# A transformer tower on one core: order of the router's preparation on TensorE and VectorE between fusion and the first expert

## The chip, the cores and the metric

One core of a Trainium2 chip runs the whole program. The time is device microseconds of that core for one launch, input in device memory to output in device memory; the median of several runs counts.

## The reference

A small vision tower in float32 over 16 images, 36 tokens each (T = 576 tokens of width 256), in five steps: patch embedding; a bidirectional minGRU stack of four layers, fused to width 256; a mixture of eight experts of which each token uses two; causal attention of 8 heads; a ternary MLP. The change lies between the fusion and the experts, where this is computed:

```python
h = h + L0_attn(layernorm(h))            # ends with: einsum(h_comb, fusion_W) + fusion_b
x = layernorm(h).reshape(T, 256)
probs = softmax(x @ gate_w.T)            # 8 experts
w, idx = top_k(probs, 2)
w = w / sum(w)
combine = zeros((T, 8)).at[rows, idx].add(w)
for each expert: acc += combine[:, e] * (silu(g) * u @ down.T)   # g, u = split(x @ up.T)
h = h + acc
```

## The kernel before, in words

Activations lie transposed: 128 partitions hold features, two blocks `k` for 256, and the free axis holds tokens. Tokens are worked in two halves of NT = 288, and where tokens must be on partitions in six tiles `j` of 96, three for each half. Every engine has an order written out by hand, and semaphores tie them together; `wait_ge(s, n)` stops the engine's queue until s has reached n. Nothing is scheduled by a tool.

A layer norm number i is a chain over four engines. `ln_mean(i)` on TensorE multiplies a half by a matrix of 1/256, so that every partition has the mean; VectorE's `ln_center(i)` (L1248) subtracts it; ScalarE's `squares(i)` (L1021) squares; `ln_square(i)` (L513) sums squares into three columns of 96 tokens; VectorE's `ln_eps(i)` (L1257) adds epsilon; GpSimd's `power(i)` (L410) raises to -0.5. For the two halves before the experts, i = LN_MOE and LN_MOE + 1, the result `rmoe` isn't multiplied into the activations: tokens are centred only, and the scale of each token is applied to its logits (`prs`) and, by ScalarE (L1080), to its row. `ln_square(i)` also waits until `s_ve` has reached i, that is until `ln_eps(i - 1)` is done; `ln_eps(i)` waits for its sums and for `power(i - 2)`.

The stretch of the change, in the order in which the engines run it:

- TensorE: `fuse(n, k)` (L598), the fusion product of half n with its k-th block of features, 4 passes for each k. The mean products of both halves (L499), `logits(0)` (L680), squares of half 0, `logits(1)`, squares of half 1, twelve transposes that put the centred tokens on partitions (L694), six products of zeros (`stay_warm`, L494), then the products of the ranks (L702 to L704), nine more products of zeros, and `gather_first` (L713).
- VectorE: `add_fused(n)` (L1358) adds the fusion into `h`; centering; the selection of two experts for each token (L1379 to L1396); the combine weights (L1401 to L1404, semaphore `s_comb`); from the ranks the seats (L1408), the row numbers `place` (L1412), and six masks `first` (L1417), with which `gather_first` picks the tokens of expert 0 by a product, without memory in between.
- ScalarE: the exponentials of the scaled logits (L1074), and six copies of the scaled token rows into `xtok` (L1080), for which `gather_first` waits.
- GpSimd: twelve indirect DMAs (L446) scatter the rows, with their combine weights behind them, to device memory; it waits for `s_place`, `s_comb` and the copies. Only behind all twelve (`s_move`) does SyncE load the rows of experts 1, 0 and 2 (L333), and behind these the up weights of expert 2 (L321).

The experts follow: `up` (L747), `down` (L764), and `turn_up(x)` (L723), which transposes the loaded rows of expert x. That of expert 1 stands in the middle of `down(0)`:

```python
for m in range(KH):
    for k in range(KI):
        last = pe.matmul(bank[:, 7, m * C:(m + 1) * C], wdn[i][:, k, m * P:(m + 1) * P], ...)
    if m == 0 and x == 0:
        turn_up(c, 1)
```

For x from 3 on, SyncE loads expert x's rows behind its down weights, which wait for the end of `down(x - 2)`.

Of the kernel before, what the change touches and what calls it, by code (L numbers as in the profile page):

```python
# [9 lines left out]
ALU = mybir.AluOpType  # L10
ACT = mybir.ActivationFunctionType
AX_X = mybir.AxisListType.X

P = 128
B, S = 16, 36
T = B * S
H = 256
# [41 lines left out]
def tower(nc, patches, w_tok, w_gru, w_fus, vecs, w_gate, w_up, w_down, w_qkv, w_gates, w_o, w_1, w_2, slots, mixed, out):  # L59
    with ExitStack() as ctx:  # L60
# [135 lines left out]
        def half(n):  # L196
            return slice(n * NT, (n + 1) * NT)
# [291 lines left out]
        def _(pe):  # L489
# [6 lines left out]
            def ln_mean(i, src):  # L496

                for k in range(KH):
                    last = pe.matmul(bank[:, mean_bank(i), 0:NT], avg[:], src[:, k, :], start=(k == 0), stop=(k == KH - 1))  # L499
                last.then_inc(s_mean, 1)  # L500
# [172 lines left out]
            fuse(1, 2)  # L673
            fuse(1, 3)
# [8 lines left out]

            pe.wait_ge(s_load["wr"], 16)
            for n in range(2):
                pe.wait_ge(s_hf, n + 1)
                ln_mean(LN_MOE + n, h[:, :, half(n)])
            logits(0)
            ln_square(LN_MOE)
            logits(1)  # L690
            ln_square(LN_MOE + 1)
            for j in range(6):
                for m in range(KH):
                    last = pe.transpose(bank[0:TT, j // 2, j % 2 * H + m * P:j % 2 * H + (m + 1) * P],  # L694
                                        xn[:, m, j * TT:(j + 1) * TT], ident[:])
                if j % 2 == 1:
                    last.then_inc(s_xtp, 1)

            stay_warm(6, 3)
# [521 lines left out]
        def _(dve):  # L1221
# [144 lines left out]
            for n in range(2):  # L1366
                ln_center(LN_MOE + n)
            ln_eps(LN_MOE)
# [4 lines left out]
            def by_tile(x):  # L1373
# [11 lines left out]
            ln_eps(LN_MOE + 1)  # L1385
# [5 lines left out]
            dve.wait_ge(s_pow, LN_MOE + 2)  # L1391
            dve.tensor_tensor(prs[:], pr[:], over(rmoe), ALU.mult).then_inc(s_max, 1)
# [7 lines left out]
            dve.wait_ge(s_exp, 1)  # L1400
            link(dve, dve.tensor_tensor(ex[:], ex[:], msk[:], ALU.mult))  # L1401
            link(dve, dve.tensor_reduce(den[:], by_tile(ex[:]), AX_X, ALU.add))
            link(dve, dve.reciprocal(den[:], den[:]))
            dve.tensor_tensor(xtok[:, :, H + 1:ROW], by_tile(ex[:]),  # L1404
                              den[:].rearrange("p (j o) -> p j o", o=1).broadcast_to([TT, 6, E]), ALU.mult).then_inc(s_comb, 1)
# [12 lines left out]

            link(dve, dve.tensor_reduce(rone[:], bank[0:1, 7, 6 * E:7 * E], AX_X, ALU.max))
# [215 lines left out]
```

## Time and profile before

| | |
|---|---|
| median of 3 runs | 430.42 us (429.53 to 431.42) |
| profiled execution, its own time | 425.62 us |
| its span, first to last instruction | 423.8 us |
| mean granted clock of TensorE | 0.974 |
| TensorE products busy | 397.4 us (94%) |
| TensorE weight loads busy | 334.1 us (79%) |
| VectorE / ScalarE / GpSimd busy | 206.1 / 147.7 / 104.1 us |

The span is that of one execution under the profiler, and the time beside it is that execution's. Busy TensorE time counts pipelined products from their start to a modelled end, so it says little on how fast it works; the clock and the chain of waits say more. The stretch of the change takes some 20 us from 120 on.

### The profile page before, as it was taken

What the parts mean: (1) busy time and instruction counts of PE and PEld (TensorE: products, weight loads), DVE (VectorE), ACT (ScalarE), POOL (GpSimd) and SP (SyncE); (2) the same over time, 40 slices, a digit from 0 to 9 for tenths busy, and PEclk for the clock granted to TensorE, in tenths of its full rate; (3) what the DMA queues carried; (4) which work ended last, traced back from release to release, by engine and by line L of the source; (5) the groups of instructions that cost most, each with busy time, mean ns of one, the idle gap of its engine ahead of it and who ended that gap; (6) DMA issues with size and microseconds to landing.
All of it is one profiled execution on the core that took longest, in us unless ns stands there. A gap on an engine that the chain in (4) does not pass through costs nothing.

```text
span 423.8 us, 6446 instructions
## 1 busy us (share of the span) xinstructions
PE 397.4 (94%) x2482; PEld 334.1 (79%) x2482; DVE 206.1 (49%) x438; ACT 147.7 (35%) x314; POOL 104.1 (25%) x126
## 2 busy tenths in 40 slices
PE   8999999999999989999899998986999888999895
PEld 5787887888778889989799898984867555679783
DVE  0347688888945334253333424320213997435452
ACT  1045666666315212121111212110164444346542
POOL 2014544454311731120202202022010040003440
PEclk9999999999996999999899999996999999999989
DMA  7999992000000247768376574013600000000001
GB/s 236 354 318 283 354 394 84 1 2 0 2 0 2 67 115 290 227 141 300 49 291 184 164 236 107 2 19 58 223 0 2 0 2 2 2 0 2 0 2 56
DMA packets 31348, 48.43 MB, mean 114 GB/s; under 512 B 2128, under 2 KB 28368, under 8 KB 29264
## 3 DMA queue, kind: packets, MB, share of 16 engines
q1 hardware_dynamic: 28944, 45.17, 32.7%
q0 software_dynamic: 2368, 2.80, 4.4%
q8 instruction: 21, 0.34, 0.3%
q14 instruction: 15, 0.12, 0.1%
HBM read 38.90 MB, written 9.05 MB: 113 GB/s over the span
## 4 chain that ended last, share of the span: by engine, by line
PE 74%; DMA 8%; DVE 7%; issue 4%; ACT 4%; SPq 2%; POOL 1%; POOLq 0%
PE bank L747 14%; PE bank L617 14%; PE bank L764 10%; DMA wg<-slots 7%; PE bank L499 6%; PE bank L494 4%; PE bank L513 4%; PE bank L973 3%; PE bank L565 2%; PE bank L832 2%; PE bank L894 2%; PE bank L598 2%; PE bank L535 2%; PE bank L959 1%; PE bank L882 1%
## 5 line engine op out<-in xcount | busy, mean ns | idle before, releaser
L747 PE MATMUL bank<-tt,wup 128*128 128x192 f32 x512 | 88.6, 331 | 0.7 <-ACT tt L1090 0.7
L747 PEld LDWEIGHTS bank<-tt,wup 128*128 128x128 f32 x512 | 84.7, 193 | 0.9 <-issue 0.9
L1428 DVE TENSOR_TENSOR scratch<-bank,scratch 128x192 f32<-128x192 f32 x64 | 22.8, 356 | 88.0 <-ACT scratch L1105 88.0
L457 POOL DMA_INDIRECT mixed<-wg,token x16 | 22.6, 1412 | 116.3 <-DVE wg L1442 113.9
L617 PE MATMUL bank<-gru_x,wg 128*128 128x288 f32 x192 | 50.8, 408 | 0.0
L1105 ACT ACTIVATE scratch<-bank 128x192 f32<-128x192 f32 x64 | 21.2, 331 | 73.0 <-PE bank L747 73.0
L410 POOL TENSOR_TENSOR rm<-ve,half_neg 96x3 f32<-96x3 f32 x24 | 21.0, 874 | 96.5 <-DVE ve L1257 89.7
L617 PEld LDWEIGHTS bank<-gru_x,wg 128*128 128x128 f32 x192 | 35.5, 190 | 8.8
L429 POOL TENSOR_TENSOR sq<-sq 128x288 f32<-128x288 f32 x14 | 26.0, 1855 | 23.9 <-ACT sq L1021 23.9
L494 PE MATMUL bank<-zero 128*128 128x288 bf16 x155 | 26.5, 323 | 4.7 <-issue 3.5
L494 PEld LDWEIGHTS bank<-zero 128*128 128x128 bf16 x155 | 16.7, 111 | 11.1 <-issue 3.7
L513 PEld LDWEIGHTS bank<-mean_h,sq 128*96 128x96 f32 x204 | 21.5, 171 | 3.0 <-DVE fbias L1337 0.5
L764 PE MATMUL bank<-gru_x,wdn 128*128 128x192 f32 x128 | 21.9, 329 | 1.3 <-DVE gru_x L1430 1.3
L764 PE MATMUL bank<-gru_y,wdn 128*128 128x192 f32 x128 | 21.8, 328 | 1.3 <-issue 1.3
L764 PEld LDWEIGHTS bank<-gru_x,wdn 128*128 128x128 f32 x128 | 20.7, 190 | 2.2 <-issue 2.2
L764 PEld LDWEIGHTS bank<-gru_y,wdn 128*128 128x128 f32 x128 | 20.7, 190 | 2.2 <-issue 2.2
L513 PE MATMUL bank<-mean_h,sq 128*96 128x1 f32 x204 | 20.5, 222 | 0.0
L1021 ACT ACTIVATE sq<-xn 128x576 f32<-128x576 f32 x8 | 5.5, 682 | 42.7 <-DVE xn L1248 42.7
L1048 ACT ACTIVATE aa<-bank,nbz 128x288 f32<-128x288 f32 x32 | 14.3, 497 | 16.6 <-PE bank L617 16.6
L1248 DVE TENSOR_TENSOR gru_y<-gru_y,bank 128x576 f32<-128x576 f32 x16 | 12.1, 753 | 15.6 <-PE bank L499 15.6
L499 PE MATMUL bank<-gru_y,avg 128*128 128x288 f32 x64 | 19.5, 427 | 0.1
L821 PE MATMUL bank<-xn,xp 128*128 128x288 f32 x64 | 16.9, 413 | 2.0 <-ACT gru_y L1141 1.2
(217 smaller groups left out, 644.0 us busy)
## 6 DMA issues: line engine op xcount, KB each, us to landing
wup<-w_up SPq DMA_DIRECT2D x8, 2048.0 KB, 8.9
wdn<-w_down SPq DMA_DIRECT2D x8, 1024.0 KB, 6.7
slots<-empty SPq DMA_DIRECT2D x2, 2385.0 KB, 20.2
wg<-w_gru SPq DMA_DIRECT2D x4, 1024.0 KB, 10.8
wup<-w SPq DMA_DIRECT2D x2, 1024.0 KB, 9.3
wg<-slots SPq DMA_DIRECT2D x16, 99.4 KB, 5.3
xp<-w_qkv SPq DMA_DIRECT2D x1, 1536.0 KB, 16.8
xp<-patches SPq DMA_DIRECT2D x2, 432.0 KB, 6.1
```

The source lines that it names most:

```text
L410: pool.tensor_tensor(root, ve[i % 2][:], half_neg[0:TT, :], ALU.pow).then_inc(s_pow, 1)
L429: pool.tensor_tensor(sq[i % 2][:, 0, :], sq[i % 2][:, 0, :], sq[i % 2][:, 1, :], ALU.add).then_inc(s_pre, 1)
L457: pool.indirect_dma_start(out=mixed, out_offset=bass.IndirectOffsetOnAxis(ap=token[i][:, u:u + 1], axis=0), in_=yw[i][:, u, :], in_offset= ...
L494: pe.matmul(bank[0:rows, b, 0:NT], zero16[:, 0:rows], zero16[:], start=True, stop=True)
L499: last = pe.matmul(bank[:, mean_bank(i), 0:NT], avg[:], src[:, k, :], start=(k == 0), stop=(k == KH - 1))
L513: last = pe.matmul(bank[0:TT, stat_bank(i), j:j + 1], sq[i % 2][:, k, j * TT:(j + 1) * TT], mean_h[:], start=(k == 0), stop=(added or k == ...
L617: last = pe.matmul(bank[:, 2 * g + m, 0:NT], wg[:, l, d, g, k, m * P:(m + 1) * P], src, start=(k == 0), stop=(k == KH - 1))
L747: last = pe.matmul(bank[:, 2 + m % 4, g * 256:g * 256 + C], wup[i][:, k, g * I + m * P:g * I + (m + 1) * P], xg[i][:, k, :], start=(k == 0 ...
L764: last = pe.matmul(bank[:, 7, m * C:(m + 1) * C], wdn[i][:, k, m * P:(m + 1) * P], act[i][:, k, :], start=(k == 0), stop=(k == KI - 1))
L821: last = pe.matmul(bank[:, head_bank(q), 0:NT], wqkv[:, k, c * 512 + m * P:c * 512 + (m + 1) * P], xn[:, k, half(n)], start=(k == 0), stop ...
L1105: sc_.activation(sg[m % 2], bank[:, 2 + m % 4, 0:C], ACT.Sigmoid).then_inc(ps[c]["sig"], 1)
L1428: dve.tensor_tensor(gt[m % 2], bank[:, 2 + m % 4, 0:C], sg[m % 2], ALU.mult).then_inc(s_vact[c], 1)
```

## The change

Three things are moved; no operation is added or removed but two of the products of zeros.

- TensorE: the mean product of half 0 goes between the last two fusion products of half 1, behind a wait for `add_fused(0)`. `logits(0)` comes ahead of the mean product of half 1; then the transposes of half 0, `logits(1)`, both squares, and the transposes of half 1. Four products of zeros follow instead of six.
- VectorE: `add_fused` and `ln_center` alternate by half. `ln_eps` of each half moves back: that of half 0 from ahead of the logits to behind the first choice, that of half 1 to behind the second mask.
- VectorE: `prs`, the scaled logits, goes behind the selection, and the four operations of the combine weights go behind the six masks.

```diff
--- before.py
+++ after.py
@@ -671,6 +671,8 @@
             fuse(1, 1)
             pe.wait_ge(s_norm, LN_MOE)
             fuse(1, 2)
+            pe.wait_ge(s_hf, 1)
+            ln_mean(LN_MOE, h[:, :, half(0)])
             fuse(1, 3)
 
             def logits(n):
@@ -681,22 +683,25 @@
                                          start=(k == 0), stop=(k == KH - 1))
                 last.then_inc(s_logit, 1)
 
+            def rows(n):
+                for j in range(n * JT, (n + 1) * JT):
+                    for m in range(KH):
+                        last = pe.transpose(bank[0:TT, j // 2, j % 2 * H + m * P:j % 2 * H + (m + 1) * P],
+                                            xn[:, m, j * TT:(j + 1) * TT], ident[:])
+                    if j % 2 == 1:
+                        last.then_inc(s_xtp, 1)
+
             pe.wait_ge(s_load["wr"], 16)
-            for n in range(2):
-                pe.wait_ge(s_hf, n + 1)
-                ln_mean(LN_MOE + n, h[:, :, half(n)])
             logits(0)
+            pe.wait_ge(s_hf, 2)
+            ln_mean(LN_MOE + 1, h[:, :, half(1)])
+            rows(0)
+            logits(1)
             ln_square(LN_MOE)
-            logits(1)
             ln_square(LN_MOE + 1)
-            for j in range(6):
-                for m in range(KH):
-                    last = pe.transpose(bank[0:TT, j // 2, j % 2 * H + m * P:j % 2 * H + (m + 1) * P],
-                                        xn[:, m, j * TT:(j + 1) * TT], ident[:])
-                if j % 2 == 1:
-                    last.then_inc(s_xtp, 1)
-
-            stay_warm(6, 3)
+            rows(1)
+
+            stay_warm(4, 3)
             pe.wait_ge(s_msk, 1)
             flat = lambda x: x[:].rearrange("p e j -> p (e j)")
             pe.matmul(bank[0:TT, 7, 0:6 * E], not_before[:], flat(msk), start=True, stop=False)
@@ -1363,9 +1368,7 @@
             dve.wait_ge(s_fb, 1)
             for n in range(2):
                 add_fused(n)
-            for n in range(2):
                 ln_center(LN_MOE + n)
-            ln_eps(LN_MOE)
 
             def over(x):
                 return x[:].rearrange("p (o j) -> p o j", o=1).broadcast_to([TT, E, 6])
@@ -1382,14 +1385,13 @@
                                                op0=ALU.is_equal, op1=ALU.mult))
             link(dve, dve.tensor_reduce(mx1[:], by_tile(keys[:]), AX_X, ALU.max))
             link(dve, dve.tensor_tensor(sel[:, 0], keys[:], over(mx1), ALU.is_equal))
-            ln_eps(LN_MOE + 1)
+            ln_eps(LN_MOE)
             link(dve, dve.scalar_tensor_tensor(out=dest[:, 0], in0=sel[:, 0], scalar=MASKED, in1=pr[:],
                                                op0=ALU.mult, op1=ALU.add))
             link(dve, dve.tensor_reduce(mx1[:], by_tile(dest[:, 0]), AX_X, ALU.max))
             link(dve, dve.tensor_tensor(keys[:], dest[:, 0], over(mx1), ALU.is_equal))
             link(dve, dve.tensor_tensor(keys[:], keys[:], ranks[:], ALU.mult))
-            dve.wait_ge(s_pow, LN_MOE + 2)
-            dve.tensor_tensor(prs[:], pr[:], over(rmoe), ALU.mult).then_inc(s_max, 1)
+            ln_eps(LN_MOE + 1)
             link(dve, dve.tensor_reduce(mx1[:], by_tile(keys[:]), AX_X, ALU.max))
             link(dve, dve.tensor_tensor(sel[:, 1], keys[:], over(mx1), ALU.is_equal))
             link(dve, dve.tensor_tensor(msk[:], sel[:, 0], sel[:, 1], ALU.add))
@@ -1397,12 +1399,8 @@
                                    msk[:].rearrange("p e j -> p (e j)"), 0.0, ALU.mult, ALU.add).then_inc(s_msk, 1)
 
 
-            dve.wait_ge(s_exp, 1)
-            link(dve, dve.tensor_tensor(ex[:], ex[:], msk[:], ALU.mult))
-            link(dve, dve.tensor_reduce(den[:], by_tile(ex[:]), AX_X, ALU.add))
-            link(dve, dve.reciprocal(den[:], den[:]))
-            dve.tensor_tensor(xtok[:, :, H + 1:ROW], by_tile(ex[:]),
-                              den[:].rearrange("p (j o) -> p j o", o=1).broadcast_to([TT, 6, E]), ALU.mult).then_inc(s_comb, 1)
+            dve.wait_ge(s_pow, LN_MOE + 2)
+            dve.tensor_tensor(prs[:], pr[:], over(rmoe), ALU.mult).then_inc(s_max, 1)
             dve.wait_ge(s_rank, 1)
             seats = bank[0:TT, 7, 0:6 * E].rearrange("p (e j) -> p e j", j=6)
             link(dve, dve.tensor_tensor(keys[:], seats, first_slot[:], ALU.add))
@@ -1416,6 +1414,12 @@
             for j in range(6):
                 dve.tensor_scalar(first[:, j, :], seat_row, seat0[:, j:j + 1], None, ALU.is_equal).then_inc(s_first, 1)
 
+            dve.wait_ge(s_exp, 1)
+            link(dve, dve.tensor_tensor(ex[:], ex[:], msk[:], ALU.mult))
+            link(dve, dve.tensor_reduce(den[:], by_tile(ex[:]), AX_X, ALU.add))
+            link(dve, dve.reciprocal(den[:], den[:]))
+            dve.tensor_tensor(xtok[:, :, H + 1:ROW], by_tile(ex[:]),
+                              den[:].rearrange("p (j o) -> p j o", o=1).broadcast_to([TT, 6, E]), ALU.mult).then_inc(s_comb, 1)
             link(dve, dve.tensor_reduce(rone[:], bank[0:1, 7, 6 * E:7 * E], AX_X, ALU.max))
             dve.tensor_scalar(flag[:], rone[:], float(C) + 0.5, None, ALU.is_gt).then_inc(s_flag, 1)
```

## Rows read from the trace of the kernel before

**Rows 1.** Chain of waits, 120 to 142 us: start us, length us, what it was.
```profile
120.35 4.41 PE bank L598 x18
...
124.78 0.95 DVE h L1358 x2
...
125.78 1.24 PE bank L499 x4
127.02 0.94 PE bank L680 x12
127.96 1.01 PE bank L513 x12
128.97 1.92 PE bank L680 x12
...
132.81 2.64 PE bank L694 x12
135.44 0.92 PE bank L494 x6
...
137.92 4.15 PE bank L713 x24
```

**Rows 2.** Chain of waits, 179 to 211 us, same columns.
```profile
179.41 5.27 DMA wg<-slots
...
185.28 5.23 PE bank L747 x32
...
203.94 6.91 PE bank L747 x32
```

**Rows 3.** Windows, TensorE: length, busy (count), granted clock, DMA share, GB/s.
```profile
127.00:128.80 1.80, 1.80 (x25) 1.00 0.00 0
128.90:135.60 6.70, 6.70 (x39) 0.50 0.01 2
```

**Rows 4.** Timeline of VectorE, 127 to 139 us: start, length, instruction, idle before it.
```profile
127.05 0.75 DVE L1248 TENSOR_TENSOR xn<-h,bank 128x576 f32<-128x576 f32 x1 [0.55 <-PE bank L499]
...
131.00 0.20 DVE L1379 TENSOR_REDUCE mx<-bank 96x6 f32<-96x48 f32 x1 [1.83 <-PE bank L680]
...
132.90 0.16 DVE L1257 TENSOR_SCALAR ve<-bank 96x3 f32<-96x3 f32 x1 [0.71 <-PE bank L513]
...
133.48 0.20 DVE L1389 TENSOR_TENSOR keys<-dest,mx 96x48 f32<-96x48 f32 x1
...
134.09 0.20 DVE L1392 TENSOR_TENSOR prs<-pr,rmoe 96x48 f32<-96x48 f32 x1 [0.17 <-POOL rmoe L410]
...
135.13 0.18 DVE L1401 TENSOR_TENSOR ex<-ex,msk 96x48 f32<-96x48 f32 x1
...
136.50 0.20 DVE L1408 TENSOR_TENSOR keys<-bank,first_slot 96x48 f32<-96x48 f32 x1 [0.43 <-PE bank L704]
...
137.02 0.32 DVE L1412 TENSOR_REDUCE place<-dest 96x12 int32<-96x96 f32 x1
...
137.45 1.46 DVE L1417 TENSOR_SCALAR wg<-wg,seat 96x192 f32<-96x192 f32 x6
```

**Rows 5.** Timeline of ScalarE, the six copies of the token rows.
```profile
134.48 2.26 ACT L1080 ACTIVATE wg<-bank,rmoe 96x256 f32<-96x256 f32 x6
```

**Rows 6.** Timeline of GpSimd, both powers and the first two scatters.
```profile
129.25 0.85 POOL L410 TENSOR_TENSOR rmoe<-ve,half_neg 96x3 f32<-96x3 f32 x1 [9.41 <-DVE ve L1257]
133.14 0.85 POOL L410 TENSOR_TENSOR rmoe<-ve,half_neg 96x3 f32<-96x3 f32 x1 [3.04 <-DVE ve L1257]
...
138.27 1.24 POOL L446 DMA_INDIRECT slots<-wg,place  x1 [3.88 <-DVE place L1412]
139.81 0.95 POOL L446 DMA_INDIRECT slots<-wg,place  x1 [0.30 <-issue]
```

**Rows 7.** SyncE's second load of expert rows: length ns, start; time to landing.
```profile
L333 SPq DMA_DIRECT2D wg<-slots x1: 427/427/427, 155.1 to 155.1; - x1
...
DMA to landing us min/median/max: 2.1/2.1/2.1
```

**Rows 8.** Timeline of TensorE's weight loads at `turn_up(1)`.
```profile
157.27 0.38 PEld L723 LDWEIGHTS bank<-ident,wg 96*128 96x128 f32 x4
```


## The prediction

> **What bounds the kernel now.** I read the chain of waits first, from the fusion products to the experts [rows 1]: TensorE works without a pause except for one handover at 124.76, then waits for VectorE before the first gather at 137.92. The chain then stays on TensorE until 179.41, where it runs through a load of expert rows [rows 2]. So the change sits on the path. The windows show the clock [rows 3]: full speed (2.4 GHz) until 128.8, granted 0.50 (1.2 GHz) from 128.9 to 135.6, after TensorE had run fusion and mean products and then the narrow products of router and squares. At half speed twelve pairs of the router take 1.92 us, at full speed 0.94 [rows 1].
>
> Beside this chain there is a second path. GpSimd's twelve scatters start at 138.27 [rows 6]. SyncE loads the rows of expert 1 behind the last of them: its second load is issued at 155.1 and lands 2.1 us later, about 157.23 [rows 7]. TensorE takes those rows at 157.27 [rows 8], without having stood still. The two paths meet with 0.04 us of slack. What the gather gains alone is therefore lost at `turn_up(1)`, in the middle of `down(0)`; what the scatters lose is paid in full, because the later row loads follow the end of `down` [rows 2].
>
> **The change, first at full clock.** The fusion's last 18 passes take 4.41, so four take 0.98 [rows 1]. The mean product of half 0, put before `fuse(1, 3)`, moves the fusion's end from 124.76 to 125.74. `add_fused(1)` takes 0.95 and the mean of half 1 1.24 [rows 1]: 128.0. Centering takes 0.75 [rows 4]: 128.8. The first six transposes lie under it: twelve took 2.64 at half clock, so six take 0.66 at full. `logits(0)` lies under the addition. `logits(1)` follows: 0.94 and some 0.2 to fill an idle engine, 129.95, and VectorE starts its maximum at 130.05 instead of 131.00 [rows 4]. That is 0.95 gained, partly because the clock had fallen before.
>
> From there VectorE runs as before: five operations from 131.00 to 132.19 (132.90 less the 0.71 idle) take 1.19 [rows 4]. Now `ln_eps(LN_MOE)` stands behind them, and `ln_square(LN_MOE + 1)` waits for it, since a square of i waits until `s_ve` is i. This is a wait that the change adds. The first squares end at 129.95 + 1.01 = 130.96 [rows 1], the epsilon at 131.40, so the second squares run from 131.45 to 132.46, and behind them wait `rows(1)`, the warm products and the ranks. VectorE's next four take 1.02 (132.90 to 134.09 less 0.17), until 132.26; `ln_eps(LN_MOE + 1)` then waits for the second squares until 132.55. The selection up to the scan takes 134.09 to 135.20, of which 0.13 was `prs`, now moved behind: 0.98 and 0.08 for the epsilon, so the scan ends at 133.61, 1.6 sooner. On TensorE six transposes end at 133.1 and four warm products near 133.7 (six took 0.92 [rows 1]; two fewer are hidden, since the scan is as late). The ranks cost between 0.14 (end of the warm products to VectorE's 136.50) and 0.45 more; I take 0.45, as nothing is queued ahead. VectorE forms the seats at 134.1, against 136.50: 2.4 sooner.
>
> Now the moved combine weights. Before, their four operations ran from 135.13 to 136.07, in the wait for the ranks, and cost nothing [rows 4]; the idle after them was 0.43. Now they follow the six masks. From seats to places is 0.84, to the first mask 0.95, the masks 1.46, the weights 0.93: 137.4. GpSimd waits for both places and weights. Before, places were last (137.34) and the first scatter began 0.93 later. Now weights are last, 2.4 to 2.5 behind places: 137.4 + 0.93 = 138.35, against 138.27. The 2.4 us won are all spent.
>
> The gather does gain: the second power is ready at 132.55 + 0.16 + 0.90 = 133.6 [rows 6], `prs` starts near 133.65; from `prs` at 134.09 to the end of the six row copies were 134.48 + 2.26 - 134.09 = 2.65 [rows 4, 5], so 136.3, and the gather starts at 136.5, 1.4 sooner. TensorE would want the rows of expert 1 at 155.85; they come at 157.3. Net at full clock against the profiled execution: +0.04, nothing.
>
> **At half clock**, if it falls near 128.9 as it did [rows 3]: `logits(1)` ends at 128.85 + 0.2 + 1.92 = 130.97, VectorE's five at 132.24. The first squares (1.9) end at 132.9, the epsilon at 133.16, the second squares at 135.1 (before: 132.81), the scan at 136.26. Six transposes at 0.22 end at 136.4, four warm products by 137.1, seats come at 137.4 (+0.9), weights at 140.75, the first scatter at 141.65: +3.4. The gather loses 1.1. Net +3.4.
>
> **Equal clocks at full speed.** The profiled execution of before is not its best. With the clock up: `logits(1)` 128.97 to 129.9, second squares 130.9, scan near 133.4, weights 134.35, twelve transposes and six warm products 133.0, seats 134.35, first scatter 134.35 + 0.84 + 0.93 = 136.1. Against 138.35 that is +2.2. So the cost is 2.2 to 3.4 wherever both kernels have the same clock, and 0 where only the changed one keeps it.
>
> **A rule against the row.** The two powers on GpSimd took 0.85 each, the first with VectorE idle, the second (133.14 to 133.99) beside VectorE's two-input operations, of which one at 133.48 took its usual 0.20 [rows 4, 6]. By this both powers may lie beside VectorE's selection for nothing, and the sum stays. The Trainium skill, "SBUF — State Buffer", section "SBUF: two separate sides", has VectorE's operations with two SBUF inputs and a GpSimd operation that reads SBUF lock one pair of ports against each other, the later one blocked. By that rule each power would hold VectorE up by at most 0.85, and the sum would be up to 1.7 more. This trace does not agree with it for these sizes.
>
> **Other unknowns.** The first scatter took 1.24, the later ones 0.95 [rows 6]; it ran beside the masks, which it no longer does: -0.3 to 0, I take 0. That TensorE stops 1.4 at `turn_up(1)` may move where the clock falls later: one stretch of 32 up products took 6.91 where the same work took 5.23 [rows 2], so -1.7 to +1.7; I take 0.
>
> **The rivals.** A, the forecast: the clock is alike in both kernels, and the weights behind the masks put the scatters later: +2.2 to +3.4. I take +2.5, nearer the full-clock sum, since that is the state of most of the span. Chance 0.50.
> B, not slower: the wide products now put among the narrow ones keep the clock up past the second squares where before it fell at 128.9: 0 to +1. For it: a mean product and six transposes now stand between the two router products. Against: the squares and `logits(1)` are still narrow and adjacent, some 3 us with the added wait. It decides from the point where seats come 2.4 us sooner. Chance 0.30.
> C, faster: B's clock, the scatter 0.3 shorter, and a later fall of the clock gone, 1.7: -2.0 or a little more. Chance 0.11.
> D, much slower: the clock falls late and comes back only inside the gather, whose 4.15 at full clock [rows 1] then cost up to 1.7 more, on top of +3.4: +5.1. Fewer warm products (four for six) speak for it; that the scatters bind and not the gather hides most of it. Chance 0.06. The port rule of above would give 2.5 + 1.7 = +4.2, chance 0.03.
>
> **The numbers.** The profiled execution took 425.62 us for a span of 423.8, 4.8 below the median of the runs, 430.42. The sum is a difference and is put on the median: 430.42 + 2.5 = 432.9 (the profiled one would be 428.1). 0.5% is 2.15 us, about what a measurement can tell from no change. Range: from B's 0 with 1.1 for the spread of the runs shown (429.3) to A's upper end, +3.4, with 1.0 (434.8); it leaves out most of C and of D. A's own range is 432.4 to 434.0. Slower by over 0.5%: A, less a little at its lower edge, and D with the port rule: 0.52. Faster: part of C, with noise: 0.09. Within: B, the rest of C and A's edge: 0.39.
>
> **What would show it.** Seats near 134.1 at full clock or 137.4 at half; the weights' four operations right behind the masks; the first scatter 0.9 behind the weights, not the places; a gap before the squares of LN_MOE + 1; TensorE idle 1 to 2 us before `turn_up(1)`, on expert rows. I am wrong if TensorE does not wait there, or if the first scatter starts before 137.

## The result, and the profile after

The changed kernel's median is 432.05 us (428.75 to 436.77, 20 runs) against 429.43 us (424.66 to 436.59, 20 runs) of the kernel before, timed side by side: a ratio of 1.0065, with a 95% interval of 1.0036 to 1.0094. That is 2.6 us slower; the forecast was 432.9 us, +2.5. Medians here take all executions; ratios and their intervals leave out those that ran some per cent longer at a lower granted clock. The profiled execution took 428.75 us for a span of 427.0. All later times are those of that execution unless a label stands beside them; lines of kernel.py have moved by up to five (the router's products L682, epsilon L1262, seats L1406, places L1410, masks L1415, ranks L707 to L709, gather L718, `turn_up` L728, `up` L752, `down` L769).

The chain of waits of the changed kernel, 123 to 166 us (start, length, what), answers to [rows 1]:

```profile
123.95 0.97 PE bank L499 x4
124.92 0.97 PE bank L598 x4
...
129.01 1.20 PE bank L682 x12
...
131.82 1.92 PE bank L513 x12
...
138.41 4.17 PE bank L718 x24
...
150.61 6.31 another core or an unknown queue
...
160.30 4.82 PE bank L769 x14
```

The handover that stood at 124.76 is filled, and `logits(1)` starts at 129.01 and ends at 130.21. In spite of that the gather starts 0.5 us later than before (138.41 against 137.92), and a piece of 6.31 us that belongs to no engine's work stands in the middle of `up(0)`; before had none. TensorE's timeline shows the added wait, and its windows (length, busy time of TensorE, weight loads, VectorE, ScalarE and GpSimd, granted clock, DMA share, GB/s) the clock, as in [rows 3]:

```profile
130.06 1.16 PE L513 MATMUL bank<-mean_h,sq 128*96 128x1 f32 x12
131.82 1.92 PE L513 MATMUL bank<-mean_h,sq 128*96 128x1 f32 x12 [0.61 <-DVE ve L1262]
```

```profile
127.00:131.90 4.90, 4.10 (x36) 3.52 (x36) 2.14 (x9) 1.97 (x2) 0.14 (x1) 1.00 0.00 0
132.00:138.70 6.70, 6.70 (x36) 5.57 (x36) 3.96 (x20) 3.49 (x8) 1.86 (x4) 0.50 0.01 2
```

The second squares waited 0.61 us for `ln_eps(LN_MOE)`, and the clock went from 2.4 to 1.2 GHz right at their start, 3.1 us later than before, for about as long as before (6.7 us). VectorE and GpSimd, against [rows 4] and [rows 6]:

```profile
130.31 0.20 DVE L1382 TENSOR_REDUCE mx<-bank 96x6 f32<-96x48 f32 x1 [1.35 <-PE bank L682]
...
131.52 0.16 DVE L1262 TENSOR_SCALAR ve<-bank 96x3 f32<-96x3 f32 x1
...
133.84 0.16 DVE L1262 TENSOR_SCALAR ve<-bank 96x3 f32<-96x3 f32 x1 [1.30 <-PE bank L513]
...
136.27 0.20 DVE L1406 TENSOR_TENSOR keys<-bank,first_slot 96x48 f32<-96x48 f32 x1 [1.10 <-PE bank L709]
...
136.79 0.32 DVE L1410 TENSOR_REDUCE place<-dest 96x12 int32<-96x96 f32 x1
...
137.22 1.46 DVE L1415 TENSOR_SCALAR wg<-wg,seat 96x192 f32<-96x192 f32 x6
138.60 0.20 DVE L1418 TENSOR_TENSOR ex<-ex,msk 96x48 f32<-96x48 f32 x1
...
139.32 0.24 DVE L1421 TENSOR_TENSOR wg<-ex,den 96x48 f32<-96x48 f32 x1
```

```profile
131.76 0.85 POOL L410 TENSOR_TENSOR rmoe<-ve,half_neg 96x3 f32<-96x3 f32 x1 [11.74 <-DVE ve L1262]
134.08 0.85 POOL L410 TENSOR_TENSOR rmoe<-ve,half_neg 96x3 f32<-96x3 f32 x1 [1.47 <-DVE ve L1262]
...
140.54 1.18 POOL L446 DMA_INDIRECT slots<-wg,place  x1 [5.21 <-DVE wg L1421]
142.02 0.96 POOL L446 DMA_INDIRECT slots<-wg,place  x1 [0.30 <-issue]
```

Seats are 0.23 sooner than before (136.27 against 136.50), the first scatter is 2.27 later (140.54 against 138.27). It now begins 4.27 us behind the seats instead of 1.77, and its releaser is the last of the moved weights' operations, no longer the places. GpSimd stood idle 5.21 us before it instead of 3.88; what the moved weights add is the 2.5 us by which the distance from the seats grew.

The wait forecast at `turn_up(1)` does not show: its products run at 165.76, right behind the first half of `down(0)`. `down(0)` was late itself, and its first half was slow:

```profile
160.30 5.46 PE L769 MATMUL bank<-gru_x,wdn 128*128 128x192 f32 x16 [6.43 <-DVE gru_x L1434]
```

```profile
160.30:165.70 5.40, 5.40 (x17) 5.31 (x18) 0.00 (x0) 0.00 (x0) 0.00 (x0) 0.50 0.97 343
```

Before, the same sixteen products took 2.84 us. Here TensorE had stood idle for 6.43 us, and the granted clock in them was 0.50. ScalarE's sigmoids in `up(0)` say why `down(0)` came late:

```profile
146.11 0.33 ACT L1110 ACTIVATE scratch<-bank 128x192 f32<-128x192 f32 x1 [0.97 <-issue]
147.70 0.33 ACT L1110 ACTIVATE scratch<-bank 128x192 f32<-128x192 f32 x1 [1.26 <-PE bank L752]
150.59 0.33 ACT L1110 ACTIVATE scratch<-bank 128x192 f32<-128x192 f32 x1 [2.56 <-PE bank L752]
156.94 0.33 ACT L1110 ACTIVATE scratch<-bank 128x192 f32<-128x192 f32 x1 [6.03 <-remote]
157.73 0.75 ACT L1110 ACTIVATE scratch<-bank 128x192 f32<-128x192 f32 x2 [0.45 <-remote]
```

They should follow each other every 1.3 us, as they did before. Instead ScalarE stands for 6.03 us although TensorE had finished all of `up(0)` at 153.87, and `down(0)` begins at 160.30. The last scatter was issued at 154.44. I had not foreseen this, so the experiments had two questions: what part of the change holds the scatters, and by which way a late scatter costs time.

### The profile page after: what moved, and what is told of

The parts are those of the page before. It is cut to its first block, busy times and chain, and to the rows that moved or that the text cites. A ratio compares the mean times of both kernels' runs of the same rounds, so it can differ in the third digit from the quotient of the medians.

```text
span 427.0 us, 6441 instructions
## 1 busy us (share of the span) xinstructions
PE 394.0 (92%) x2480; PEld 332.2 (78%) x2480; DVE 206.0 (48%) x438; ACT 147.6 (35%) x314; POOL 104.3 (24%) x126
## 4 chain that ended last, share of the span: by engine, by line
PE 72%; DMA 8%; DVE 7%; issue 4%; ACT 4%; SPq 2%; another core or an unknown queue 2%; POOL 1%; POOLq 0%; DVEq 0%
PE bank L617 14%; PE bank L752 13%; PE bank L769 11%; DMA wg<-slots 6%; PE bank L499 6%; PE bank L494 4%; PE bank L513 4%; PE bank L565 2%; PE bank L978 2%; PE bank L837 2%; PE bank L899 2%; PE bank L598 2%; PE bank L535 1%; PE bank L887 1%
## 5 line engine op out<-in xcount | busy, mean ns | idle before, releaser
L752 PE MATMUL bank<-tt,wup 128*128 128x192 f32 x512 | 86.9, 327 | 0.7 <-ACT tt L1095 0.7
L752 PEld LDWEIGHTS bank<-tt,wup 128*128 128x128 f32 x512 | 83.1, 190 | 0.9 <-issue 0.9
L457 POOL DMA_INDIRECT mixed<-wg,token x16 | 22.6, 1413 | 120.9 <-DVE wg L1446 118.5
L769 PE MATMUL bank<-gru_x,wdn 128*128 128x192 f32 x128 | 24.6, 354 | 6.4 <-DVE gru_x L1434 6.4
L494 PE MATMUL bank<-zero 128*128 128x288 bf16 x153 | 25.0, 312 | 4.9 <-issue 3.6
L769 PEld LDWEIGHTS bank<-gru_x,wdn 128*128 128x128 f32 x128 | 23.1, 208 | 7.3 <-issue 7.3
L494 PEld LDWEIGHTS bank<-zero 128*128 128x128 bf16 x153 | 15.8, 107 | 10.2 <-issue 3.9
L769 PE MATMUL bank<-gru_y,wdn 128*128 128x192 f32 x128 | 21.8, 328 | 1.3 <-issue 1.3
L769 PEld LDWEIGHTS bank<-gru_y,wdn 128*128 128x128 f32 x128 | 20.7, 190 | 2.2 <-issue 2.2
```

The lines of the kernel that those rows point to most:

```text
L457: pool.indirect_dma_start(out=mixed, out_offset=bass.IndirectOffsetOnAxis(ap=token[i][:, u:u + 1], axis=0), in_=yw[i][:, u, :], in_offset= ...
L494: pe.matmul(bank[0:rows, b, 0:NT], zero16[:, 0:rows], zero16[:], start=True, stop=True)
L752: last = pe.matmul(bank[:, 2 + m % 4, g * 256:g * 256 + C], wup[i][:, k, g * I + m * P:g * I + (m + 1) * P], xg[i][:, k, :], start=(k == 0 ...
```

## The experiments

Each group ran on a chip of its own, interleaved with the kernel before. Before's medians were 429.29 us (35 runs) beside the first group, 422.75 us (29) beside the second and 430.1 us (29) beside the third. All kernels compute the whole reference.

### First group: which part costs

`r_after` is the changed kernel again.

> The changed kernel once more, for a second profile. In its first profile ScalarE stood still for 6.0 us in the middle of up(0) (150.9 to 156.9), with its inputs ready. If that stall belongs to the change, it is there again at the same sigmoid. If it is an accident of one execution, ScalarE runs every 1.3 us there, and TensorE waits instead at turn_up(1) for the rows of expert 1, 1 to 2 us. The first scatter starts 3.1 to 3.3 us behind VectorE's seats minus places, that is 4.2 us behind the seats (before: 1.8). Time against before: +0.3 to +1.0%.

Measured: 430.48 us, ratio 1.0047 (1.0009 to 1.0085). Here the clock stayed up through the second squares, so this is the forecast's full-clock walk as a measurement:

```profile
130.34 0.20 DVE L1382 TENSOR_REDUCE mx<-bank 96x6 f32<-96x48 f32 x1 [1.35 <-PE bank L682]
...
133.93 0.26 DVE L1398 TENSOR_TENSOR_SCAN incl<-tile_reset,msk 96x48 bf16<-96x48 bf16 x1
...
134.68 0.20 DVE L1406 TENSOR_TENSOR keys<-bank,first_slot 96x48 f32<-96x48 f32 x1 [0.25 <-PE bank L709]
...
137.74 0.23 DVE L1421 TENSOR_TENSOR wg<-ex,den 96x48 f32<-96x48 f32 x1
```

The first scatter starts at 138.95: 4.27 behind the seats again. The gather starts at 136.93 but takes 6.15 us instead of 4.15: the window from 137 to 142.5 has a mean granted clock of 0.64. The stall was there again: ScalarE stood 5.27 us, until its sigmoid at 155.89, and `down(0)` began at 160.36.

`e_comb_early` is the changed kernel with the weights back ahead of the ranks.

```diff
             dve.tensor_tensor(prs[:], pr[:], over(rmoe), ALU.mult).then_inc(s_max, 1)
+            dve.wait_ge(s_exp, 1)
+            link(dve, dve.tensor_tensor(ex[:], ex[:], msk[:], ALU.mult))
...
             dve.wait_ge(s_rank, 1)
```

> The changed kernel with one thing undone: the four operations of the combine weights stand ahead of the wait for the ranks again, behind prs. Theory (the weights behind the masks put the scatters later): the first scatter starts 1.8 us behind the seats instead of 4.2, so 2.4 us sooner than in the changed kernel at the same clock; the time falls to before or below it, -0.5 to 0%, 2 us less than the changed kernel. Rival (TensorE's order costs, by the wait for ln_eps or by the clock): the time stays where the changed kernel's is, +0.3 to +0.9%.

Measured: 431.72 us, ratio 1.0017 (0.9965 to 1.0068). Seats 135.27, first scatter 137.03, so 1.76 behind the seats: the 2.5 us of distance belong to the weights' place and to nothing else. They are not all won back, though. The weights now stand ahead of the seats and hold them up: from VectorE's maximum to the seats are 5.28 us (4.34 in `r_after`), and from the maximum to the first scatter 7.04 (8.61 in `r_after`). So putting the weights back is worth 1.6 us at this clock, not the 2.4 expected. The median does not come down, the ratio does; this group alone does not settle the time. The stall is here too, but TensorE has work in it, and the first half of `down(0)` keeps its speed:

```profile
158.13 2.84 PE L769 MATMUL bank<-gru_x,wdn 128*128 128x192 f32 x16 [1.29 <-DVE gru_x L1434]
```

`e_comb_late` is the kernel before with only that one move.

```diff
-            dve.wait_ge(s_exp, 1)
-            link(dve, dve.tensor_tensor(ex[:], ex[:], msk[:], ALU.mult))
...
             for j in range(6):
                 dve.tensor_scalar(first[:, j, :], seat_row, seat0[:, j:j + 1], None, ALU.is_equal).then_inc(s_first, 1)
+            dve.wait_ge(s_exp, 1)
+            link(dve, dve.tensor_tensor(ex[:], ex[:], msk[:], ALU.mult))
...
```

> The kernel before with one thing done: the four operations of the combine weights stand behind the six masks. Theory: the first scatter starts 4.2 us behind the seats instead of 1.8, but the seats can come up to 0.9 us sooner where the ranks are ready before the weights end; +1.5 to +2.4 us, +0.35 to +0.55%. Rival (TensorE's order costs): 0 within 0.2%.

Measured: 429.94 us, ratio 1.0047 (1.0005 to 1.0088). Up to the scan its timeline of VectorE is also the kernel before's at a full clock:

```profile
130.14 0.20 DVE L1379 TENSOR_REDUCE mx<-bank 96x6 f32<-96x48 f32 x1 [0.94 <-PE bank L680]
...
132.54 0.20 DVE L1392 TENSOR_TENSOR prs<-pr,rmoe 96x48 f32<-96x48 f32 x1 [0.17 <-POOL rmoe L410]
...
134.16 0.20 DVE L1402 TENSOR_TENSOR keys<-bank,first_slot 96x48 f32<-96x48 f32 x1 [0.50 <-PE bank L704]
...
134.68 0.32 DVE L1406 TENSOR_REDUCE place<-dest 96x12 int32<-96x96 f32 x1
```

With the clock up VectorE's maximum is at 130.14 in the old order and 130.34 in the new. The "0.95 gained" of the forecast was all clock. What the kernel before does at this clock can be worked out from it. The scan starts at 133.41, and the ranks are ready at 134.16. With the weights in their old place the seats stand 1.03 behind the scan where nothing waits (133.24 and 134.27 in `e_ranks_first`). That gives seats at 134.44 and the first scatter 1.77 later, at 136.2; here it starts at 138.42. Against `r_after`'s 138.95 the whole change costs the scatters 2.7 us where both clocks are up until the squares are through, 2.2 of them for the weights' place and 0.5 for the new orders of the rest. These sums rest on one profile of each kernel.

The same profile answers for the gather. `prs` is at 132.54 here and at 134.23 in `r_after`, since the change puts it behind the selection, and ScalarE's six copies of the rows wait for it. They end at 135.19 here and at 136.88 in `r_after`, and the gather follows at 136.02 and 136.93. At equal clocks the changed kernel's gather is thus not sooner but some 0.9 us later.

`e_te_only` has TensorE's new order and VectorE's old one.

```diff
             fuse(1, 2)
+            pe.wait_ge(s_hf, 1)
+            ln_mean(LN_MOE, h[:, :, half(0)])
             fuse(1, 3)
...
             logits(0)
-            ln_square(LN_MOE)
+            pe.wait_ge(s_hf, 2)
+            ln_mean(LN_MOE + 1, h[:, :, half(1)])
+            rows(0)
             logits(1)
+            ln_square(LN_MOE)
             ln_square(LN_MOE + 1)
```

> TensorE's order of the changed kernel with VectorE's order of before, so that ln_eps of half 0 stands ahead of the logits and no wait is added for the second squares. Theory: the weights are ready in the wait for the ranks, the first scatter starts 1.8 us behind the seats; -2 to 0 us, -0.45 to 0%. Rival (TensorE's order costs): +0.3 to +0.9%.

Measured: 431.34 us, ratio 1.0061 (1.0021 to 1.0102). The expectation missed how the two orders mesh. TensorE waits 1.79 us for the centering before `logits(0)` (127.69, since both additions now come first), and VectorE's maximum waits behind `ln_eps(LN_MOE)`, whose squares now stand behind `logits(1)`: 133.08 instead of 130.34. Seats come at 137.64, the first scatter 1.77 behind them at 139.41. The expectation of -0.45 to 0% was missed. The two orders are worth something only together; as a split of the cost this run says nothing.

### Second group: how a late scatter costs

`r_before` is the kernel before under a second name, to see how far apart two timings of one kernel lie.

> The kernel before once more, for a second profile. Five of six profiles so far (all but the one of before) show ScalarE standing still for 4 to 6 us inside up(0) while the scatters run, and going on as they end. Theory 1: the stall belongs to the stretch and comes in before's executions too; down(0) then starts about 20 us behind the first scatter, near 156 to 158, not at 154.7. Theory 2: the stall belongs to the change (or to what it shares with its parts); then it is absent here again and ScalarE runs every 1.3 us. If the clock holds through the second squares, the first scatter starts near 136.0 (138.3 at half clock). Time: 0 within 0.4%.

Measured: 421.92 us, ratio 0.9955 (0.9915 to 0.9996). The interval leaves out 1 for the same kernel. Ratios here are thus good to about 0.5%, not to the 0.4% that their intervals show, and I rest no verdict on a single one below that. First scatter 137.89, gather 137.72, sigmoids every 1.3 us, `down(0)` at 154.28, `turn_up(1)` at 157.12 without a wait.

`x_scatter_late` is the kernel before with the scatters held until all sigmoids of expert 0 are done.

```diff
             pool.wait_ge(s_id, 2)
+            pool.wait_ge(ps[0]["sig"], KI)
             for j in range(6):
```

> The kernel before, with GpSimd's scatters held until ScalarE has done its eight sigmoids of up(0). If the scatters in flight are what holds ScalarE up, its sigmoids run every 1.3 us here without a stall, and the stall may show up later, beside the scatters. If not, the stall of 4 to 6 us stands in up(0) as before. The time is some 12 to 17 us longer, as the rows of expert 1 come that much later.

Measured: 443.35 us, one run. Its chain of waits:

```profile
168.52 2.42 DMA slots<-wg,place
170.95 0.34 SPq L333
...
171.34 2.10 DMA wg<-slots
...
173.48 0.90 PE bank L724 x4
174.39 4.08 PE bank L765 x16
```

Scatters, landing, row load and `turn_up(1)` follow each other without a gap. First scatter 16.8 us later, `turn_up(1)` 16.4 us later, the whole some 20 us slower (12 to 17 were expected): the second path of the forecast, at its full price once its slack is gone. Some 2 us of the rest lie right there: the granted clock was 0.50 from 165 to 173.4, while TensorE stood idle, and `turn_up(1)` and the sixteen products behind it took 0.90 and 4.08 us instead of 0.35 and 2.63. ScalarE did not stall, but no kernel of this group did, so this run doesn't say whether the scatters cause the stall.

`e_turn_late` is the changed kernel with `turn_up(1)` behind `down(0)` instead of in its middle.

```diff
-                    if m == 0 and x == 0:
-                        turn_up(c, 1)
                 last.then_inc(ps[c]["dmm"], 1)
+                if x == 0:
+                    turn_up(c, 1)
```

> The changed kernel with turn_up(1) behind down(0) instead of in its middle. That gives the scatters 2.6 us more and costs about 1 us at the start of up(1), where TensorE waits for ScalarE's copy. If TensorE waits at turn_up(1) for the rows, this takes 1 to 1.5 us off the changed kernel. If ScalarE's stall sets the start of down(0) and the rows are there by then, it adds 1 us: +0.2 to +0.3% on the changed kernel.

Measured: 424.51 us, ratio 1.005 (1.0016 to 1.0084). Without a stall its timeline of TensorE reads:

```profile
153.59 5.44 PE L769 MATMUL bank<-gru_x,wdn 128*128 128x192 f32 x32 [1.30 <-DVE gru_x L1434]
158.87 0.50 PE L728 MATMUL bank<-ident,wg 96*128 96x96 f32 x4
159.99 2.84 PE L752 MATMUL bank<-tt,wup 128*128 128x192 f32 x16 [0.62 <-issue]
...
177.95 1.46 PE L752 MATMUL bank<-tt,wup 128*128 128x192 f32 x8
```

The gather began 1.0 us sooner than in `r_before` (136.72 against 137.72) and `down(0)` 0.7 sooner, and after two experts TensorE is 0.13 us behind it (the last row is at 177.82 there). That lead is one of clocks: in `r_before` the clock had fallen at 130.2, here at 133.5, and at equal clocks there is none (`e_comb_late`). It is lost here all the same, though not by the forecast's wait: the first scatter is at 138.78, so by [rows 6, 7] the rows are there at about 157.7, before `turn_up(1)` at 158.87. In its place TensorE stands 0.62 us between the turned rows and their first product. In the unmoved order TensorE would have wanted them at 153.59 + 2.84 = 156.4 and stood 1.3 us; that is worked out, and no profile shows it.

The unmoved changed kernel did not run on this chip, so the ratio says what this kernel costs and not what the move of `turn_up(1)` is worth.

`e_no_eps_wait` is `e_comb_early` without the added wait of the second squares.

```diff
                     pe.wait_ge(s_sq, i + 1)
-                if i >= 1:
+                if i >= 1 and i != LN_MOE + 1:
                     pe.wait_ge(s_ve, i)
```

> The changed kernel with the combine weights back ahead of the ranks, and without the wait of the second squares for ln_eps of the first half (they write another bank than the first). Theory: the 0.6 us of TensorE idle before the second squares is gone, the selection ends 0.5 us sooner, and the first scatter starts 0.4 to 0.6 us sooner than in the kernel with the weights alone put back (137.0 at full clock): 136.5. Still 0.5 behind before at the same clock (136.0). Time: -0.4 to +0.2% against before.

Measured: 421.41 us, ratio 0.9981 (0.9948 to 1.0015). Both squares are now one stretch of 24 products and VectorE doesn't idle at the second epsilon:

```profile
130.18 2.18 PE L513 MATMUL bank<-mean_h,sq 128*96 128x1 f32 x24
```

```profile
133.51 0.25 DVE L1398 TENSOR_TENSOR_SCAN incl<-tile_reset,msk 96x48 bf16<-96x48 bf16 x1
...
135.21 0.19 DVE L1412 TENSOR_TENSOR keys<-bank,first_slot 96x48 f32<-96x48 f32 x1
```

The scan is 0.4 us sooner than in `r_after` (133.51 against 133.93), so the added wait was worth that much. The seats are not sooner, since the weights, now ahead of them, wait for the exponential behind `prs`. First scatter 136.97, where 136.5 was expected.

### Third group: the same again on a third chip, and a version of my own

`r_after2`, `e_comb_early2` and `e_comb_late2` are `r_after`, `e_comb_early` and `e_comb_late` unchanged.

> The changed kernel a third time. On the chip of the second group no kernel showed ScalarE's stall, on that of the first group all did. Without the stall: TensorE waits at turn_up(1) for rows, 1.3 to 2 us; first scatter 4.2 us behind the seats (138.9 at full clock through the squares, up to 141 with the clock down); +0.4 to +0.8% against before. With the stall: down(0) starts near 160 again.

> The weights back ahead of the ranks, again, beside the changed kernel on one chip. Theory (the weights' place is the main cost): 1.9 us before the changed kernel at the same clock, scatter 1.8 behind the seats; -0.1 to +0.3% against before, and below the changed kernel by 0.3 to 0.5%. Rival (TensorE's order is the main cost): within 0.1% of the changed kernel.

> The kernel before with the weights alone moved behind the masks, again. Theory: its first scatter stands 4.2 us behind the seats; the wait at turn_up(1) is there with TensorE's old order too, 2 us at full clock; +0.4 to +0.5%. Rival: 0 within 0.2%.

Measured: `r_after2` 431.54 us, 1.0024 (0.9989 to 1.006); `e_comb_early2` 431.48 us, 0.9968 (0.9925 to 1.001); `e_comb_late2` 432.74 us, 1.0019 (0.9975 to 1.0062). The profiled execution of `e_comb_early2` took 437.46 us at a granted clock of 0.959, so only distances inside it are read. In `r_after2` the clock was down from the second squares on, as in the changed kernel's first profile. The whole stretch lies 1.6 us later than in `r_after`, since fourteen fusion products ahead of it took 4.51 us instead of 3.42 (maximum at 131.96 against 130.34), so it is read from the maximum on:

```profile
133.48 2.05 PE L513 MATMUL bank<-mean_h,sq 128*96 128x1 f32 x12 [0.61 <-DVE ve L1262]
```

```profile
138.05 0.20 DVE L1406 TENSOR_TENSOR keys<-bank,first_slot 96x48 f32<-96x48 f32 x1 [1.10 <-PE bank L709]
```

```profile
142.33 1.18 POOL L446 DMA_INDIRECT slots<-wg,place  x1 [5.21 <-DVE wg L1421]
...
156.19 0.94 POOL L446 DMA_INDIRECT slots<-wg,place  x1 [0.30 <-issue]
```

`e_ranks_first` is the kernel before with the rank products put ahead of the last four transposes, and without the six warm products.

```diff
-            stay_warm(6, 3)
+            rows(range(4))
             pe.wait_ge(s_msk, 1)
...
             pe.matmul(bank[0:TT, 7, 6 * E:7 * E], ones16[:], incl[:, :, 5], start=True, stop=True).then_inc(s_rank, 1)
+            rows(range(4, 6))
```

> The kernel before, with the products of the ranks ahead of the last four transposes and without the six products of zeros. In both profiles of before VectorE stood 0.4 and 1.0 us before the seats, since TensorE was still at transposes and zeros. Theory (the scatters set the pace): the seats come right behind the weights, the first scatter 0.4 to 1.0 us sooner, and the gather, which then waits for the later row copies, no later than before; -0.25 to -0.1%. If the missing zeros let the clock stay down in the gather, up to +0.5%.

Measured: 426.17 us in six runs, ratio 0.99 (0.9844 to 0.9956), four times the most that was expected and the only one below before by more than two timings of one kernel differ. The ranks are out of the queue's way:

```profile
130.74 1.89 PE L695 MATMUL bank<-ident,xn 128*96 128x128 f32 x8
133.55 0.27 PE L703 MATMUL bank<-msk,not_before 96*96 96x48 bf16 x1 [0.92 <-DVE incl L1398]
```

```profile
133.41 0.18 DVE L1403 TENSOR_TENSOR ex<-ex,msk 96x48 f32<-96x48 f32 x1
...
134.12 0.23 DVE L1406 TENSOR_TENSOR wg<-ex,den 96x48 f32<-96x48 f32 x1
134.27 0.19 DVE L1410 TENSOR_TENSOR keys<-bank,first_slot 96x48 f32<-96x48 f32 x1
```

TensorE now waits 0.92 us for the scan, where the old order made VectorE wait for TensorE. The weights fill the ranks' time, the seats follow them at once, and the first scatter starts at 136.03. That is 6.06 us behind the maximum, against 7.27 and 7.66 in the two profiles of before, and 6.1 worked out above for before at a full clock: what the new place of the ranks saves is the wait for TensorE at the low clock. The run changes two things, the place of the ranks and the six products of zeros, and does not tell them apart; nor do the 1.2 to 1.6 us explain all of the 1%.

### What the runs say together

| | maximum | clock falls at | seats | first scatter | behind seats |
|---|---|---|---|---|---|
| before | 131.00 | 128.9 | 136.50 | 138.27 | 1.77 |
| `r_before` | 130.23 | 130.2 | 136.12 | 137.89 | 1.77 |
| `e_comb_early` | 129.99 | 133.7 | 135.27 | 137.03 | 1.76 |
| `e_no_eps_wait` | 130.43 | 133.1 | 135.21 | 136.97 | 1.76 |
| `e_ranks_first` | 129.97 | 130.8 | 134.27 | 136.03 | 1.76 |
| `e_te_only` | 133.08 | 134.3 | 137.64 | 139.41 | 1.77 |
| `e_comb_late` | 130.14 | 132.2 | 134.16 | 138.42 | 4.26 |
| `e_turn_late` | 130.13 | 133.5 | 134.51 | 138.78 | 4.27 |
| `e_comb_late2` | 129.86 | 129.6 | 135.93 | 140.21 | 4.28 |
| `r_after` | 130.34 | 134.1 | 134.68 | 138.95 | 4.27 |
| changed | 130.31 | 132.0 | 136.27 | 140.54 | 4.27 |
| `r_after2` | 131.96 | 133.4 | 138.05 | 142.33 | 4.28 |

Where the clock falls is worked out from windows of 2 to 3.5 us (the mean of 1.00 before the fall and 0.50 after it).

The distance has two values, and only the place of the weights decides which: 2.5 us. Of these the seats give back up to 0.9 where the ranks are ready before the weights would be. In time, over the two chips that ran all three, the mean ratio is 1.0036 for the changed kernel, 1.0033 for the kernel before with the weights moved alone, and 0.9993 for the changed kernel with them moved back. Each of these is inside the 0.5% that two timings of one kernel differ by; that they fall as the profiles say is support, not proof. So is this: on each of the two chips the ratios rise with the first scatter of the kernel's profile. Scatters at 137.03, 138.42, 138.95 and 139.41 go with ratios of 1.0017, 1.0047, 1.0047 and 1.0061 in the first group, and 136.03, 138.37, 140.21 and 142.33 with 0.99, 0.9968, 1.0019 and 1.0024 in the third.

The stall of ScalarE showed in all nine profiles of the first and third group and of the changed kernel, and in none of the second group nor of the kernel before's first. Where it showed, its end followed the scatters. Of the sigmoids held back, the last started between 3.07 and 3.36 us after the twelfth scatter was issued (`r_after` 152.82 and 155.89, `e_comb_early` 150.96 and 154.10, `e_comb_late` 152.31 and 155.45, changed 154.44 and 157.73, `r_after2` 156.19 and 159.55, `e_ranks_first` 149.96 and 153.24 are six of the nine). `down(0)` then starts 19.6 to 22.6 us behind the first scatter, against 16.4 in `r_before`. So on such a chip a later scatter mostly delays `down(0)` itself: it began at 157.27 in `e_ranks_first`, at 159.93 in `e_comb_late2` and at 162.12 in `r_after2`. The tie is loose, though. `e_comb_early` and `e_comb_late` have their scatters 1.4 us apart and begin `down(0)` at 158.13 and 158.02.

| | first up product to `down(0)` | first half of `down(0)` |
|---|---|---|
| the five profiles without the stall | 11.93 or 11.94 | 2.84 (`e_turn_late`: both halves in 5.44) |
| `e_comb_early` | 14.76 | 2.84 |
| `e_ranks_first` | 15.31 | 2.84 |
| `e_te_only` | 15.82 | 2.84 |
| `e_comb_early2` | 18.11 | 4.74 |
| `r_after` | 16.63 | 5.04 |
| changed | 17.07 | 5.46 |
| `r_after2` | 17.27 | 5.46 |
| `e_comb_late` | 17.43 | 5.24 |
| `e_comb_late2` | 17.76 | 4.72 |

The stall makes `up(0)` 2.8 to 6.2 us longer. In all five profiles of the lower rows, those with the weights late, and in `e_comb_early2`, the clock was also down in the first half of `down(0)`, which then took 1.9 to 2.6 us more; in the other three it was not. So a late scatter can cost time on these chips in a second way. Of this the forecast has only the open term for a later fall of the clock, taken at 0.

## Why the prediction was right, step by step

**The result's kind and size.** +2.5 us forecast, +2.6 measured beside it, +1.2 and +1.4 in the two repeats. Slower by over 0.5% had most of the chance, and the first ratio lies there; the repeats (1.0047, 1.0024) put the truth near the bound between "slower" and "no change". The mean of the three is 1.0045. The place of the weights was foreseen and measured; the way from the scatters to the time was not the one forecast, so that the size fits to 0.1 us is in part luck.

**The full-clock walk** held with an error of 0.6 us that arose early and was carried on. `logits(1)` ended 0.3 late (VectorE's maximum 130.34 for 130.05), the second squares started 0.4 late (131.87 for 131.45), the scan ended 0.6 late (134.19 for 133.61), seats 134.68 for 134.1, first scatter 138.95 for 138.35. **The half-clock walk** did not occur as a whole: in no profile was `logits(1)` of the changed kernel at half clock. From the maximum on it did. There the forecast had 6.3 us to the seats (131.07 to 137.4; 4.05 at full clock), and measured are 5.96 and 6.09 in the first profile and `r_after2`, 4.34 in `r_after`. With the maximum 0.7 sooner than that walk had it, the first scatter of the changed kernel's first profile, 140.54, lies between the two walks' 138.35 and 141.65. The kernel before at full clock was put at 136.1, and `e_comb_late` gives 136.2. So "+2.2 at equal full clocks" is 2.7: the mis-sized terms are the start of `logits(1)` behind the second centering and what the added wait adds to it.

**The moved weights.** "4.2 behind the seats, before 1.8" measured 4.27 and 1.77 in the changed kernel and the kernel before, and 4.26 to 4.28 or 1.76 to 1.77 in every other profile but that of `x_scatter_late`, whose scatters were held. This is the step that carried the forecast, and `e_comb_late` shows it alone.

**"0.95 gained" before the selection** was right as a difference of two executions (0.69 in the first profile) and wrong as a gain of the order, which is -0.2 at equal clock (130.34 for 130.14). The prediction said "partly"; it was all.

**The added wait** stood where it was put, 0.61 us, and cost the scan 0.4 (`e_no_eps_wait`).

**The gather sooner, and lost again.** With the clock up through the squares it started at 136.72 to 136.93 (forecast 136.5), 0.8 to 1.0 sooner than in `r_before`. But the forecast took its "1.4 sooner" against an execution whose clock had fallen at 128.9. The old order with the clock up through the squares started the gather at 136.02 (`e_comb_late`), and there the change makes it 0.9 later, because `prs` and with it the row copies stand behind the selection. So this step failed too. The loss was forecast at `turn_up(1)`, on expert rows, and the prediction named it as its test: "I am wrong if TensorE does not wait there". TensorE did not wait there in any profile of the changed kernel. That step failed. In three of them ScalarE's stall came first, 5 to 6 us inside `up(0)`, and was over only after the last scatter, when the rows were close behind. In `e_turn_late`, without the stall, `turn_up(1)` had been moved. That the price of late scatters was still about right has this reason: both ways hang on the end of the scatters. That the half-clock start of `down(0)` comes on top on one side, and that the tie to the scatters is loose on the other, makes the agreement luck as well. `x_scatter_late` shows that the forecast's way exists; that it would have bound an unmoved and unstalled changed kernel by 1.3 us was only argued.

**The clock (B and C).** It fell 3.1 us later in the first profile and later still in `r_after` and `r_after2`, but in `e_comb_late`, with the old order, too (132.2). It differs from execution to execution in both kernels, so neither B's case nor the forecast's "alike" is a property of the kernel. Where it fell late it was still low in the gather: 6.15 us for 4.15 in `r_after`, 6.03 in `e_comb_early`. That is D's mechanism, and its part of 1.7 was 2.0; D's place for it, on top of the half-clock walk, did not occur. It came with the full-clock walk instead, whose sum had no such term.

**The powers beside VectorE** took 0.85 each, beside VectorE's operations of 0.20 to 0.23 us as usual. By the Trainium skill's "SBUF — State Buffer", section "SBUF: two separate sides", the one that started later should have been blocked; for tiles of 96x3 and 96x48 the trace does not agree, before or after. The first scatter took 1.18 instead of 1.24, so the "-0.3 to 0" was -0.06.

## What to carry to other kernels

Work that stands in a wait is free only there: before moving it behind the wait, look who else waits for its result, here GpSimd for four operations of 0.9 us that had lain under the ranks and then put its first scatter 1.6 to 2.5 us later, masks included. What gains is the reverse: put the products that another engine is waiting for ahead of those nobody waits for yet (`e_ranks_first`, 1.0% below before in six runs on one chip). And take differences between two profiles only at the same clock: the same kernel gave a first scatter at 138.95 and at 140.54 from the same start of the selection (130.34 and 130.31).

## What the runs showed of the hardware that I had not expected

- On two of the chips ScalarE stood for 3 to 6 us among the sigmoids, while GpSimd's scatters ran and its own inputs lay ready; on a third chip, and in the first profile of the kernel before, it never did. The profile names no source ("remote", "an unknown queue"). The end of the stall is tied to the last scatter within 0.3 us over nine profiles, its cause is open: the one kernel that kept scatters and sigmoids apart ran on the chip that has no stall, and I did not try it on another.
- The kernel before had a median of 422.75 us on the chip without the stall and of 429.29 and 430.1 on the two with it. It was not profiled on those two, so whether the 7 us are the stall is not shown. The stall made `up(0)` 2.8 to 6.2 us longer where it was seen, so it could be most of them. That before's one profile without it took 425.62 us, less than 19 of the 20 timings beside the changed kernel, also fits.
- The second of two timings of an identical kernel came out at 0.9955 with an interval that left out 1.
